# Norm bound for a softmax shift: squares of two head groups added on GpSimd, two selector products per chunk, shift constant 38

## The reference

```python
x = x + xattn(layernorm(x), ctx_1024, ctx_1024, Wq, bq, Wk, bk, Wv, bv, Wo, bo)
x = x + ffn(layernorm(x), W_experts, b_experts, W_router, b_router)

# xattn, E = 32
q = (queries @ Wq + bq).reshape(B, L, H, E)     # keys, values likewise
scores = jnp.einsum('blhe,bshe->bhls', q, k)
A = jax.nn.softmax(scale * scores, axis=-1)     # scale = 1 / sqrt(E)
out = jnp.einsum('bhls,bshd->blhd', A, v).transpose(0, 2, 1, 3).reshape(B, L, H * E)
return out @ Wo + bo
```

## Time and profile before

| | us |
| --- | --- |
| median of 3 runs (2332.82 to 2336.57) | 2333.98 |
| the profiled execution | 2331.29 |
| its span, first to last instruction | 2329.5 |
| PE busy | 2257.5 (97%) |
| DVE busy | 2026.0 (87%) |
| ACT busy | 1841.8 (79%) |
| POOL busy | 746.2 (32%) |

### The profile page before, as it was taken

The page is one execution under the profiler, slowest core; times in us unless marked ns, Lnnn a source line. Parts: engine busy times, 40 slices in busy tenths (PEclk is TensorE's granted clock), DMA queues, the critical chain, the costliest instruction groups (busy, mean ns, idle before and its releaser), DMA issues. The chain is left out here.

```text
span 2329.5 us, 49256 instructions
## 1 busy us (share of the span) xinstructions
PE 2257.5 (97%) x19592; PEld 1084.2 (47%) x19592; DVE 2026.0 (87%) x1831; ACT 1841.8 (79%) x2125; POOL 746.2 (32%) x826
## 2 busy tenths in 40 slices
PE   8999899999999999999999999999999999789999
PEld 7878633333333333333333333333333357578777
DVE  4358589999999999999999999999999989866565
ACT  3213399999999999999999999999999976534333
POOL 2212223232232332232233332322323323245655
PEclk9999899999999999999999999999999999889999
DMA  7436564445564555557566774656654468634464
GB/s 264 163 137 216 187 163 111 108 106 121 126 176 110 121 126 130 136 135 209 129 147 151 159 142 121 172 129 150 149 121 104 99 179 283 212 105 138 144 203 142
DMA packets 149435, 350.75 MB, mean 151 GB/s; under 512 B 33078, under 2 KB 65814, under 8 KB 131932
## 3 DMA queue, kind: packets, MB, share of 16 engines
q0 software_dynamic: 51328, 202.69, 36.7%
q1 hardware_dynamic: 95548, 137.33, 18.3%
q10 hardware_dynamic: 2336, 7.60, 1.1%
HBM read 147.68 MB, written 99.56 MB: 106 GB/s over the span
## 5 line engine op out<-in xcount | busy, mean ns | idle before, releaser
L1175 ACT ACTIVATE probs<-psum 128x1536 f32<-128x1536 f32 x800 | 1159.2, 1449 | 0.0
L1332 PE MATMUL psum<-probs,v_st 128*32 128x512 f32 x6400 | 852.1, 605 | 0.2 <-ACT probs L1175 0.2
L1282 PE MATMUL psum<-q_st,k_st 32*128 32x512 f32 x9600 | 779.1, 425 | 20.8 <-ACT probs L1175 13.1
L1282 PEld LDWEIGHTS psum<-q_st,k_st 32*128 32x128 f32 x9600 | 397.6, 183 | 713.3 <-ACT probs L1174 376.1
L1240 DVE TENSOR_TENSOR even_sums<-even_sums,probs 128x2048 f32<-128x2048 f32 x287 | 654.4, 2280 | 34.6 <-ACT probs L1175 31.7
L1240 DVE TENSOR_TENSOR odd_sums<-odd_sums,probs 128x2048 f32<-128x2048 f32 x256 | 584.3, 2283 | 0.1
L1174 ACT ACTIVATE probs<-psum 128x512 f32<-128x512 f32 x800 | 478.0, 597 | 38.1 <-PE psum L1282 33.9
L1332 PEld LDWEIGHTS psum<-probs,v_st 128*32 128x32 f32 x6400 | 126.0, 108 | 290.5 <-issue 281.4
L2129 PE MATMUL psum<-we_hi,wo 128*128 x624 | 219.6, 413 | 7.9 <-DVE wo L2020 6.1
L980 POOL DMA_DIRECT2D pile<-probs x96 | 88.5, 922 | 249.6 <-DMA pile<-probs 167.8
L959 POOL CAST rest_split<-rest_probs 72x512 fp32r<-72x512 f32 x32 | 38.1, 1192 | 379.8 <-ACT rest_probs L1145 379.8
(11 more groups left out here) (226 smaller groups left out, 2376.3 us busy)
## 6 DMA issues: line engine op xcount, KB each, us to landing
pile<-probs POOLq DMA_DIRECT2D x128, 1024.0 KB, 7.5
token_rows<-rows SPq DMA_DIRECT2D x8, 1028.0 KB, 6.8
xn<-in_x SPq DMA_DIRECT2D x16, 512.0 KB, 6.5
q_st<-qh_scratch SPq DMA_DIRECT2D x32, 256.0 KB, 4.9
q_st<-ql_scratch SPq DMA_DIRECT2D x32, 256.0 KB, 5.6
token_rows<-in_x SPq DMA_DIRECT2D x8, 1024.0 KB, 10.8
biased_rows<-in_bo POOLq DMA_DIRECT2D x8, 1024.0 KB, 21.0
xb<-biased_rows SPq DMA_DIRECT2D x32, 256.0 KB, 4.3
```

Of the source, the lines that this page charges most:

```text
L1175: act.activation(probs[:, p, 1:HG, :], psum[:, bank(it, t, 1):bank(it, t, 1) + HG - 1, :], ACT.Exp, bias=-WIDEST, scale=SCALE).then_inc(ex ...
L1282: return nc.tensor.matmul(psum[:, bank(it, t, h), :], k_st[rows, part, t * P:(t + 1) * P], q_st[it % 2][rows, of, :], start=start, stop=stop)
L1332: mm = nc.tensor.matmul(psum[h * DH:(h + 1) * DH, bank, :], lhs(h), rhs(h), start=start, stop=stop)
```

## The change

POOL no longer squares each group into its own slot. For a pair of groups, (0, 1) and (2, 3), it squares both into `each` and adds the two into `squares[:, n]`, so a chunk has four squares and two additions. PE has two products per chunk in place of four, and `of_head` has two blocks. Every head of group 0 thereby shares its sum with a head of group 1, and of group 2 with one of group 3: eight sums, each of two heads' squared norms. The result is still a bound, but a larger one. `WIDEST` becomes 38, in the comparison and as the constant of the exponentials. The addition waits for both squares, and the squares of the next pair wait for the addition, since `each` has one buffer. The wait for PE's sum of the chunk before has moved from the first square to the first addition. The fold compares and inverts in one step in place of two.

```diff
-WIDEST = 30.0
+WIDEST = 38.0
+PAIRS = ((0, 1), (2, 3))
...
-        squares = sb("squares", [P, NG, CH], F32R)
-        of_head = sb("of_head", [P, NG, P], F32R)
+        each = sb("each", [P, 2, CH], F32)
+        squares = sb("squares", [P, len(PAIRS), CH], F32R)
+        of_head = sb("of_head", [P, len(PAIRS), P], F32R)
...
-                    for j in range(NG):
-                        pool.wait_ge(hi, c * NG + (j + 1))
-                        if j == 0 and summed is not None:
+                    for n, pair in enumerate(PAIRS):
+                        if n:
+                            pool.wait_ge(squared, c * len(PAIRS) + n)
+                        elif before and isinstance(c, int) and c == 0:
+                            pool.wait_ge(k_squared, before * len(PAIRS))
+                        elif summed is not None:
+                            pool.wait_ge(squared, c * len(PAIRS))
+                        for u, j in enumerate(pair):
+                            pool.wait_ge(hi, c * NG + (j + 1))
+                            h = o_hi[b][:, j, 0:w].bitcast(F32)
+                            pool.tensor_tensor(each[:, u, 0:w], h, h, ALU.mult).then_inc(parts_squared, 1)
+                        pool.wait_ge(parts_squared, before * NG + c * NG + (pair[-1] + 1))
+                        if n == 0 and summed is not None:
                             pool.wait_ge(*summed)
-                        h = o_hi[b][:, j, 0:w].bitcast(F32)
-                        pool.tensor_tensor(squares[:, j, 0:w], h, h, ALU.mult).then_inc(squared, 1)
+                        pool.tensor_tensor(squares[:, n, 0:w], each[:, 0, 0:w], each[:, 1, 0:w], ALU.add).then_inc(squared, 1)
...
-                for j in range(NG):
+                for n, pair in enumerate(PAIRS):
                     for h in range(HG):
-                        dve.memset(of_head[h * DH:(h + 1) * DH, j, HG * j + h:HG * j + h + 1].bitcast(F32), 1.0).then_inc(selector, 1)
+                        spots = of_head[h * DH:(h + 1) * DH, n, 0:HEADS].rearrange("p (j h) -> p j h", h=HG)
+                        dve.memset(spots[:, pair[0]:pair[-1] + 1, h].bitcast(F32), 1.0).then_inc(selector, 1)
...
-                dve.tensor_scalar(too_wide[:], widest[:], (WIDEST / SCALE) ** 2 / SLACK, None, ALU.is_le).then_inc(fold, 1)
+                dve.tensor_scalar(too_wide[:], widest[:], (WIDEST / SCALE) ** 2 / SLACK, 0.0, ALU.is_le, ALU.is_equal).then_inc(fold, 1)
                 dve.wait_ge(fold, 5)
-                dve.tensor_scalar(too_wide[:], too_wide[:], -1.0, 1.0, ALU.mult, ALU.add).then_inc(fold, 1)
+                dve.tensor_copy(unbounded[:], too_wide[:]).then_inc(fold, 1)
...
-                    pe.wait_ge(squared, (c + 1) * NG)
-                    for j in range(NG):
-                        mm = pe.matmul(psum[:, bank, 0:w], of_head[:, j, :], squares[:, j, 0:w], start=j == 0, stop=j == NG - 1)
+                    pe.wait_ge(squared, (c + 1) * len(PAIRS))
+                    for n in range(len(PAIRS)):
+                        mm = pe.matmul(psum[:, bank, 0:w], of_head[:, n, :], squares[:, n, 0:w], start=n == 0, stop=n == len(PAIRS) - 1)
```

More of the change, by code:

```diff
@@ L216, in projections @@
         selector = sem("selector")
+        parts_squared = sem("parts_squared")
         k_squared = sem("k_squared")
@@ L345, in _, with square @@
                                    base=0, pattern=[[-1, P]], channel_multiplier=1).then_inc(ident_ready, 1)
-                def square(c, b, w, hi, squared, summed):
-                    for j in range(NG):
-                        pool.wait_ge(hi, c * NG + (j + 1))
-                        if j == 0 and summed is not None:
+                def square(c, b, w, hi, squared, summed, before):
+                    for n, pair in enumerate(PAIRS):
[11 more added lines that the diff above has]
+                        if n == 0 and summed is not None:
                             pool.wait_ge(*summed)
-                        h = o_hi[b][:, j, 0:w].bitcast(F32)
-                        pool.tensor_tensor(squares[:, j, 0:w], h, h, ALU.mult).then_inc(squared, 1)
-                square(0, 0, CH, k_hi, k_squared, None)
+                        pool.tensor_tensor(squares[:, n, 0:w], each[:, 0, 0:w], each[:, 1, 0:w], ALU.add).then_inc(squared, 1)
+                square(0, 0, CH, k_hi, k_squared, None, 0)
                 pool.wait_ge(w_in[2], 16)
@@ L360, in _ @@
                 with pool.Fori(0, pairs - 1) as i:
[L361 to L365, removed]
+                    square(i * 2 + 1, 1, CH, k_hi, k_squared, (k_summed, i * 2 + 1), 0)
+                    square(i * 2 + 2, 0, CH, k_hi, k_squared, (k_summed, i * 2 + 2), 0)
+                square(NSC - 2, 1, CH, k_hi, k_squared, (k_summed, NSC - 2), 0)
+                square(NSC - 1, 0, last_w, k_hi, k_squared, (k_summed, NSC - 1), 0)
+                square(0, 0, CH, q_hi, q_squared, (k_summed, NSC), NSC)
                 with pool.Fori(0, NC // 2 - 1) as i:
-                    square(i * 2 + 1, 1, CH, q_hi, q_squared, (q_summed, i * 2 + 1))
-                    square(i * 2 + 2, 0, CH, q_hi, q_squared, (q_summed, i * 2 + 2))
-                square(NC - 1, 1, CH, q_hi, q_squared, (q_summed, NC - 1))
+                    square(i * 2 + 1, 1, CH, q_hi, q_squared, (q_summed, i * 2 + 1), NSC)
+                    square(i * 2 + 2, 0, CH, q_hi, q_squared, (q_summed, i * 2 + 2), NSC)
+                square(NC - 1, 1, CH, q_hi, q_squared, (q_summed, NC - 1), NSC)
             @block.scalar
@@ L587, in _ @@
                 dve.wait_ge(fold, 4)
-                dve.tensor_scalar(too_wide[:], widest[:], (WIDEST / SCALE) ** 2 / SLACK, None, ALU.is_le).then_inc(fold, 1)
+                dve.tensor_scalar(too_wide[:], widest[:], (WIDEST / SCALE) ** 2 / SLACK, 0.0, ALU.is_le, ALU.is_equal).then_inc(fold, 1)
                 dve.wait_ge(fold, 5)
-                dve.tensor_scalar(too_wide[:], too_wide[:], -1.0, 1.0, ALU.mult, ALU.add).then_inc(fold, 1)
+                dve.tensor_copy(unbounded[:], too_wide[:]).then_inc(fold, 1)
                 dve.wait_ge(fold, 6)
-                dve.tensor_copy(unbounded[:], too_wide[:]).then_inc(fold, 1)
-                dve.wait_ge(fold, 7)
             @block.tensor
@@ L650, in _ @@
                 pe.wait_ge(w_lo_ready, 2)
-                pe.wait_ge(selector, 1 + HEADS)
+                pe.wait_ge(selector, 1 + HG * len(PAIRS))
                 def ctx_pair(i, w_next):
```

## The result

| kernel | median us | runs | lowest to highest | ratio to before (95% interval) |
| --- | --- | --- | --- | --- |
| before | 2334.57 | 7 | 2332.82 to 2336.57 | |
| changed | 2345.15 | 7 | 2341.32 to 2347.8 | 1.0043 (1.0033 to 1.0052) |

The account below looks back on a forecast made before the run. It took PE, busy throughout most of the projections, as the bound. -6.0 + 4.6 + 1.7 + 0.8 + 0.1 = +1.2 us gave 2335.2 us against the median of 2333.98, no change that can be told; range 2329.5 to 2339.5.

Parts of the forecast that it names:

- signs of being wrong: First chunk's wait under 3 us, clock falling for longer than 3.4 us or not at all, or query period staying at 13.83.
- the forecast 13.37: Query chunks: PE's period was to fall from 13.83 to 13.37 us, two products or 0.46 us fewer.
- Which branch, the constant, the rest of the kernel: Attention: the larger bound, 34.8 against 37.6, keeps the short branch; exponentials with another constant cost nothing.
- The gain, -6.0 us: PE in the projections: 26 products fewer at 0.23 us each, over 6 key and 7 query chunks.
- The first key chunk, +4.6: PE waits for POOL: 2.3 us for additions and waits, 2.3 more while DVE's a_lo blocks POOL; bounds 2.3 and 4.9.
- The clock behind it, +1.7: After PE's first wait: 3.4 us of work at half clock loses 1.7 us; bounds 0 and 3.4.
- Rival 4: Longer idle stretches at three PE waits cost the clock twice as long: slower, 2339.2 us; chance 0.11.
- The short key chunk, +0.8: DVE's normalising of the first query rows meets additional POOL operations: 0.8 us; bounds 0.1 and 1.1.
- The query chunks, 0: POOL's addition falls into DVE's normalising, but DVE's stock covers it over six chunks: 0; bounds 0 and 1.5.
- a stock of 2.1 us: Query chunks: normalised rows are ready 3.1 us before PE turns them, less two cuts of 0.46.
- Rival 5: DVE becomes the bound of the query chunks, locked with POOL's last square and addition: 2337.9 us; chance 0.06.
- The end, +0.1: The later last sum is mostly hidden behind SP's wait for a store: 0.1 us; bounds 0 and 0.5.

Follow-up runs that it names:

- e4_only_38: The kernel before with only the constant 38 in place of 30; 2335.14 us against 2334.9, ratio 1.0001.
- e6_keys_only: Changed kernel with additions only in key chunks 1 to 5, four squares and four products in all other chunks; 2333.91 us, ratio 0.9998 to before.
- e2_no_add: Changed kernel without the additions, only the second square of each pair summed, so half of each bound left out; 2331.39 us, ratio 0.9991 to before.
- e11_low_part_waits: Changed kernel, but DVE's a_lo of key chunk 1 waits until POOL has made both sums of key chunk 0; 2343.56 us, ratio 1.0042 to before.
- e1_wait_first: Changed kernel with POOL's wait for PE's sum put back to the first square of a chunk; 2341.33 us, ratio 1.0029 to before.
- e7_search_early: Changed kernel with POOL's wait back at the first square and, in query chunks, DVE's search ahead of o_lo 1; 2338.21 us, ratio 1.0014 to before.
- e3_chunk0_four: Changed kernel, but key chunk 0 has four squares, four products and no addition; 2337.77 us, ratio 1.0012 to before.
- e5_query_four: Changed kernel, but query chunks have four squares, four products, no addition, and wait at the first square; 2339.47 us, ratio 1.002 to before.
- e8_late_add_search: Changed kernel without additions in first, short key and last query chunks, wait at first square, later second query addition, earlier search; 2328.95 us, ratio 0.9978 to before.
- e10_before_search: The kernel before with only DVE's search moved ahead of o_lo 1 in the query chunks; 2333.45 us against 2333.91, ratio 0.9997.
- e9_late_add_only: Changed kernel without additions in first, short key and last query chunks, wait at first square, later second query addition, search unmoved; 2331.83 us, ratio 0.999 to before.

## Why the prediction was wrong, step by step

One of the prediction's own signs of being wrong came: the clock fell for longer than 3.4 us. The query period did not stay at 13.83 us, but it moved away from the forecast 13.37, to 14.39.

**Which branch, the constant, the rest of the kernel.** Right: e4_only_38.

**The gain, -6.0 us.** The step that failed is the 7 query chunks. 0.46 us per chunk is right in the key chunks (e6_keys_only: 2.2 us for five). In the query chunks it is nothing, even with no addition at all (e2_no_add, period 13.82). I had read "PE busy in 13.83 of 13.83" as the bound. It was one of two ways of nearly the same length: the other, over o_hi 1, o_lo 1 and the search into the turn, came 0.17 us behind in the weight loads' waits. Its length does not depend on how many products the sum has. Missing here: 3.2 us.

**The first key chunk, +4.6.** Right in mechanism and nearly in size: 5.0 us. The rest is the two additions, which take 1.26 to 1.29 us with nothing beside them, where I had taken the square's 1.04. The rule of the Trainium skill, SBUF — State Buffer, section Who interferes with whom, that whichever issues first has the shared ports for the whole instruction, is borne out: 4.18 us for two squares with a_lo issued 0.01 us ahead, 2.04 without (e11_low_part_waits), and there 6.62 instead of 2.29 us for a_lo issued 0.07 us behind `w_lo_q`.

**The clock behind it, +1.7.** Right in kind, about right in effect. The stretch was 6.8 us, twice the one that I had taken. But its first 1.9 us fell into the wait itself: from 31.62 to 55.75 PE needed 24.1 us for the 96 products that took 22.4 from 26.67 to 49.07 before, 1.7 us more. That the size agrees is luck. Rival 4 said that the longer waits cost the clock twice as long, and at the first two waits they did. But of the 6.6 us shown of each stretch PE was busy in only 4.7, so it did not cost the 3.4 us more that rival 4 gave it.

**The short key chunk, +0.8.** The normalising took 2.27 us instead of 2.00, so 0.3 us and not 0.8; but PE's first query product slipped by 1.5 us against the sum before it (161.37 to 170.60, for 157.06 to 164.79), and the way from there to the sum of query chunk 0 took 20.54 us for 19.92, behind it a low clock that lasted twice as long. Together that is 2.1 us. Of the 1.5 us the other 1.2 are in the store that ACT waits for. It took 4.8 us to land where it took 3.5 before; from the lists of transfers (KB each, us from issue to landing) of the kernel before and of the changed one:

```profile
kl_scratch<-o_lo SPq DMA_DIRECT2D x1, 260.0 KB, 3.5
```

```profile
kl_scratch<-o_lo SPq DMA_DIRECT2D x1, 260.0 KB, 4.8
```

It took 4.7 to 4.8 us in four profiles (the changed kernel, e1_wait_first, e7_search_early, e11_low_part_waits) and 3.4 to 3.9 in the nine others. The four are those with additions in key chunk 0, in the short key chunk and in the query chunks at once; e3_chunk0_four and e5_query_four have them in the short key chunk too and took 3.4 and 3.8. What decides it stays open; no experiment was made on it.

**The query chunks, 0.** This is the largest miss. From the sum of chunk 0 to that of chunk 6 it is 87.26 us for 82.96, +4.3 instead of -2.8: 7.1 us. 2.8 of them are the gain that did not come, counted above already; 4.3 are new. For these, two steps failed. First, I counted one new meeting and there were two: the wait for PE's sum, moved to the addition, let the next chunk's first square run into the normalising. I had named this move in the text on the change and didn't ask what it lets go earlier; e1_wait_first gives back 3.8 us. Second, I gave DVE a stock of 2.1 us, from the normalised rows to their use. That stock could not be used: DVE's search stands in the same list behind these rows, and PE waits for it in every chunk, 0.17 us even before. What DVE really had was its wait of 1.05 us for o_hi 1, where I had read 0.78 in the row at 199.46. One meeting more (e1_wait_first, 3.62 us for the four operations in place of 2.64) fits into it, and the period stays at 13.83; two (4.37 us, 1.73 more) don't. Rival 5 had the right engine, with a chance of 0.06 and a price cut down by that stock.

**The end, +0.1.** Within its bounds, at 0.4: from the last query sum in the loop to the first product of attention, 18.33 us for 17.91. PE's wait was 3.33 us, where rival 4 had 3.0, and the start of attention did not move with it: 8.88 us behind the last sum in place of 9.35. That SP's wait for the store hides it was read from the rows before, not tested.

**Sum.** In the profile: 6.2 up to key chunk 1 (5.0 and 1.7, less 0.5 for the two products of the sum of chunk 1; those of chunk 0 ran at the low clock and saved nothing), 1.9 less over the next four key chunks, 2.1 around the first query product, 4.3 in the query chunks, 0.4 at the end, and 2.4 at the start of attention, most of it by the clock's own variation. That makes the 13.5 of the table. The medians differ by 10.6: the profiled execution of before, 2331.29 us, is 3.3 under its median, and its short stretch of low clock at the start of attention is worth 1.7 against most other profiles.

## What to carry to other kernels

An engine that is busy all the time is the bound only if no other way beside it has the same length: look at the shortest waits for it, in the weight loads too, before a removed instruction is counted as gain. When a wait is moved, ask what runs earlier for it and whom that meets; an engine with idle time can still cost the engine that it takes turns with. An operation that is hidden in every regular turn of a loop is to be priced by itself in the first turn, where its inputs come all at once.

## What the runs showed of the hardware that I had not expected

- On POOL, adding two different tiles of 128x512 takes 1.26 to 1.30 us, squaring one (both operands the same) 1.04 (L365 and L361 in the same rows). Whether the operation or the second operand makes the difference no run separates.
- POOL and DVE take turns by the instruction: four normalising operations of 0.46 us each at a time with three POOL operations among them take 4.37 us, with two 3.62, with one 2.53 to 2.97, with none 1.92 (e8_late_add_search, e10_before_search).
- The low clock is not fixed by the length of the wait. At the first query product idle times of 3.10 and 3.17 us were followed by none (e3_chunk0_four, e6_keys_only), 2.98 by 3.4 us at 1.2 GHz (before, e8_late_add_search), 3.31 by 6.8 (e9_late_add_only), 4.35 by 3.4 (e1_wait_first) and 4.46 by 6.8 (the changed kernel). Behind the first sum it was 6.8 us after 3.86 to 5.58 of idle time and 10.2 after 5.95 (e5_query_four); the start of attention had 13.7, 17.1 or 20.5 us. One profile alone is good for 1.7 us there and not for less.
